# Causal attention with 8-wide heads on one core: queries and keys as two float32r parts in two 64-row halves, in place of three bf16 parts in 72 rows

## The chip, the cores and the metric

The kernel runs on one core of a Trainium2 chip. The metric is device time in microseconds; the figure given for a kernel is the median of its runs.

## The reference, cut to what matters

The program is a network of four stages in a row: an attention-like scan (attn_a), a feed-forward layer with local attention (ffn), the attention treated here (attn_b), and the second ffn layer; each adds to the same activations X of 4 batches by 1024 tokens by 128 channels. In attn_b, X is first normalised over the channels. Then, for 16 heads of 8 channels:

```python
Q = split_heads(einsum('bsd,od->bso', x, Wq)); K = ...; V = ...     # 16 heads of 8
Q, K = _apply_rope(Q, cos, sin), _apply_rope(K, cos, sin)
logits = einsum('bhnd,bhmd->bhnm', Q, K) / sqrt(8)                  # 1024 x 1024 for each head
logits = where(causal, logits, -inf)
probs = softmax(logits, axis=-1)
attn = einsum('bhnm,bhmd->bhnd', probs, V)
return einsum('bsd,od->bso', merge_heads(attn), Wo)
```

The logits must be near float32 precision, while a TensorE pass in bf16 keeps 8 bits of each factor. So the kernel splits each query and key into parts and sums the products of the parts along the rows (the contraction) of one matmul.

## The kernel before, in words

The 4 x 16 heads are treated in 16 groups of 4 heads (`NG`, `BG`). Each of the five engines has its own instruction stream, written out by hand in one order; semaphores hold the streams together. Nothing is scheduled at run time.

**Parts.** After projection and rotation, the queries and keys of a batch are split into three bf16 parts: ScalarE writes the first part (`first_part`, L1789), the remainder is formed (L1928 on VectorE for batch 0, L2036 on GpSimd for the others), ScalarE writes the second part (`second_part`, L1793), and the third is remainder minus second (`third_part`, L1933, L2041). The parts go to DRAM (`store_parts`), and are read back for each group with the repetitions that a matmul needs (`load`, L1505 and L1511, 3 DMAs of 192 KB each for queries and keys): 3 x 3 x 8 = 72 rows, for 4 heads by 1024 columns. Three further rows hold ones on the key side and, on the query side, the negated row maximum in three bf16 parts.

**Two score passes for each group.** The *maximum pass* (`max_unit`) makes query tile i (128 queries) against keys in pieces of up to 512 columns (L1652), with a causal mask added by a matmul with the identity (L1649) where the piece touches the diagonal, in one of two 512-column PSUM buffers (`s1_ps`). VectorE reduces each unit to a maximum (L1956). There are 38 units to a group. When a group's maxima are there, VectorE takes the minimum of the two halves (L1966), GpSimd splits it in three (L2063 to L2069), TensorE turns it (`turn_unit`, L1661), VectorE copies it out (L1973), and one DMA puts it into the query rows (`rows`, L1532). The *exponential pass* (`exp_unit`) makes key tile j against all later queries (L1684, 75 rows, so that the maximum is already subtracted), one head of up to 1024 columns at a time for j < 4 and two or four heads for shorter ones, in one of two 1024-column PSUM buffers (`s2_ps`); ScalarE evaluates the exponential into `PT` (L1867). There are 22 units to a group. In groups 0 to 2 the diagonal is masked by a matmul (L1679), from group 3 on (`SELECTS`) by a GpSimd select on `PT` (L2080). Then `value_block` (L1702) multiplies the probabilities by the values, in float32, in four 32-column strips of the array, one for each head. A ones column in the values gives the denominators.

**The order.** Step n has 8 slots. In slot j, TensorE makes the exponential units of key tile j of group n, between them the maximum units of group n+1 (slots 0 to 3) or n+2 (slots 4 to 7) in the order of tiles `MAX_TILES = (4, 7, 6, 5, 3, 2, 1, 0)`, and the value blocks of key tile j-1. `turn_unit` stands in slot 5. A maximum unit waits until VectorE has read the buffer before last (`s1_read`), an exponential unit until ScalarE has (`probs`):

```python
wait(pe, s1_read, k - 1)      # max_unit
wait(pe, probs, k - 1)        # exp_unit
if (j, g) == (0, 0):
    pe.wait_ge(s_rows[n % 2], 16 * (n // 2 + 1))
```

SyncE's queue issues, in step n: the outputs of the step before, `rows(n + 1)`, the outputs' first half, and `load(n + 3)`.

## Time and profile before

| | us |
|---|---|
| median of 3 runs | 2247.53 |
| the runs | 2243.55 to 2248.66 |
| span of the profiled execution, first to last instruction | 2242.3 |
| what the runs have around that span | 1.3 to 6.4 (5.2 at the median) |
| attn_b, within the span | 893 to 1503 |

The profiled execution's own device time is not given apart from its span. In the rows below, PE is TensorE's matmuls, PEld its weight loads, DVE VectorE, ACT ScalarE, POOL GpSimd, SPq the DMA queue of SyncE. A float32 matmul stands in the trace as two records, each with its own weight load. PEclk is the granted clock of TensorE as a share of full speed.

### The profile page before, as it was taken

Reading aid. Unit: us, or ns where it says so; the run is one execution under the profiler, and the core shown is the slowest. Engines: PE = TensorE matmul, PEld = TensorE weight load, DVE = VectorE, ACT = ScalarE, POOL = GpSimd, SP = SyncE. Lnnn points to the kernel's source line nnn. Section 1 sums busy time; section 2 is a strip of 40 time slices with the busy share of each in tenths; the row PEclk is TensorE's granted clock in tenths of the full one; section 3 lists DMA queues with packets and bytes.
Section 4 is the critical chain, followed back from the end, with each engine's and each line's share of the span. In section 5 each row is a group of like instructions: output and inputs, shape, how many; then the busy total and the mean of one; then the engine's idle time right before and its main releaser. Section 6 shows DMA issues by size and latency. Waiting matters only on the chain. (4 is left out here: it accounts for less than half of the span.)

```text
span 2242.3 us, 44709 instructions
## 1 busy us (share of the span) xinstructions
PE 2064.8 (92%) x16567; PEld 1059.9 (47%) x16567; DVE 1792.0 (80%) x2386; ACT 1390.5 (62%) x3475; POOL 1233.3 (55%) x633
## 2 busy tenths in 40 slices
PE   5677899999999997899999999967999999999997
PEld 2224555555555553443333333314555555555554
DVE  6986889899899993666777777717899899899993
ACT  8455566666666664446666666665666756766663
POOL 0217777777777772135121221128777787777770
PEclk9899999999999999889999999999999999999998
DMA  2004112112112110402111111113111111111111
GB/s 62 0 6 121 35 34 47 35 34 48 35 36 47 35 34 19 130 29 88 55 48 52 54 36 46 32 55 87 31 43 42 35 44 39 34 44 39 35 34 43
DMA packets 86075, 101.14 MB, mean 45 GB/s; under 512 B 13817, under 2 KB 59841, under 8 KB 83557
## 3 DMA queue, kind: packets, MB, share of 16 engines
q1 hardware_dynamic: 83429, 96.58, 16.8%
q8 instruction: 135, 2.21, 0.4%
q10 hardware_dynamic: 2432, 1.70, 0.3%
q14 instruction: 79, 0.65, 0.1%
HBM read 35.98 MB, written 8.39 MB: 20 GB/s over the span
## 5 line engine op out<-in xcount | busy, mean ns | idle before, releaser
L831 POOL TENSOR_TENSOR ffn_RN<-ffn_SS,ffn_mhalf 128x16 f32<-128x16 f32 x128 | 372.5, 2910 | 279.3 <-DVE ffn_SS L777 278.9
L1956 DVE TENSOR_REDUCE attn_b_NX<-attn_b_s 128x1 f32<-128x512 f32 (+3 forms) x608 | 381.3, 660 | 132.0 <-PE attn_b_s L1652 126.8
L825 POOL TENSOR_TENSOR ffn_QK<-ffn_T 128x1024 f32<-128x1024 f32 x128 | 421.6, 3294 | 17.6 <-DVE ffn_T L725 17.4
L576 ACT ACTIVATE ffn_PB<-ffn_s,ffn_NM 128x128 f32<-128x128 f32 x1024 | 360.8, 386 | 101.1 <-DVE ffn_NM L747 101.1
L1867 ACT ACTIVATE attn_b_PT<-attn_b_s 128x1024 f32<-128x1024 f32 (+3 forms) x352 | 298.2, 870 | 192.4 <-PE attn_b_s L1684 188.0
L612 ACT ACTIVATE ffn_SQ<-ffn_w 128x1024 f32<-128x1024 f32 x128 | 131.2, 1025 | 312.0 <-DVE ffn_T L725 311.7
L819 POOL TENSOR_TENSOR ffn_PB<-ffn_PB,ffn_RDEN 128x1024 f32<-128x1024 f32 x128 | 243.7, 1904 | 25.1 <-DVE ffn_RDEN L710 25.1
L367 PE MATMUL ffn_w<-ffn_Wqkv,ffn_H 128*128 128x512 f32 x512 | 244.2, 600 | 10.4 <-ACT ffn_SQ L612 4.7
L576 ACT ACTIVATION_READ_ACCUMULATOR ffn_PB<-ffn_s,ffn_NM 128x1 f32 x1024 | 231.0, 226 | 0.0
L1652 PE MATMUL attn_b_s<-attn_b_KS,attn_b_QS 72*128 72x512 bf16 (+3 forms) x768 | 220.6, 336 | 6.2 <-DVE attn_b_NX L1956 5.5
L741 DVE TENSOR_TENSOR ffn_QK<-ffn_QK,ffn_RN 128x1024 f32<-128x1024 f32 x128 | 222.4, 1738 | 0.4 <-POOL ffn_RN L831 0.3
L764 DVE COPY ffn_PT<-ffn_w 128x1024 f32<-128x1024 f32 x128 | 156.2, 1220 | 76.1 <-PE ffn_w L421 72.6
L2080 POOL TENSOR_SCALAR_AFFINE_SELECT attn_b_PT<-attn_b_PT 128x512 f32<-128x512 f32 x104 | 66.8, 642 | 252.6 <-ACT attn_b_PT L1867 251.4
L1684 PE MATMUL attn_b_s<-attn_b_QS,attn_b_KS 75*128 75x512 bf16 (+3 forms) x768 | 186.9, 333 | 5.9 <-ACT attn_b_PT L1867 4.8
L442 PE MATMUL ffn_m<-ffn_HN,ffn_W 128*114 128x512 f32 x360 | 185.9, 613 | 6.4 <-ACT ffn_G L596 3.7
L722 DVE TENSOR_TENSOR ffn_T<-ffn_w,ffn_rope 128x1024 f32<-128x1024 f32 x128 | 154.8, 1210 | 36.6 <-PE ffn_w L367 36.4
L1702 PE MATMUL attn_b_o<-attn_b_PT,attn_b_VQ 128*32 128x512 f32 (+3 forms) x1536 | 166.2, 505 | 3.8 <-POOL attn_b_PT L2080 3.5
L725 DVE TENSOR_TENSOR ffn_T<-ffn_w,ffn_rope 128x512 f32<-128x512 f32 x256 | 163.7, 681 | 0.0
L747 DVE TENSOR_REDUCE ffn_NM<-ffn_s 128x8 f32<-128x1024 f32 x128 | 155.6, 1215 | 9.6 <-PE ffn_s L409 9.6
L774 DVE TENSOR_REDUCE ffn_SS<-ffn_SQ 128x16 f32<-128x1024 f32 x128 | 154.6, 1208 | 2.2 <-ACT ffn_SQ L612 2.2
L437 PEld LDWEIGHTS ffn_w<-ffn_PT,ffn_Voff 128*64 128x64 f32 x2048 | 107.3, 137 | 100.7 <-issue 94.4
L421 PEld LDWEIGHTS ffn_w<-ident,ffn_PB 128*128 128x128 f32 x1024 | 117.4, 143 | 75.4 <-issue 60.5
(257 smaller groups left out, 3756.4 us busy)
## 6 DMA issues: line engine op xcount, KB each, us to landing
ffn_Voff<-ffn_Vcur SPq DMA_DIRECT2D x248, 128.0 KB, 2.3
attn_b_QS<-attn_b_qk_parts SPq DMA_DIRECT2D x48, 192.0 KB
attn_b_KS<-attn_b_qk_parts SPq DMA_DIRECT2D x48, 192.0 KB
ffn_H<-ffn_Y SPq DMA_DIRECT2D x64, 128.0 KB, 2.5
ffn_H<-ffn_U SPq DMA_DIRECT2D x64, 128.0 KB, 2.5
attn_b_qk_parts<-attn_b_RP SPq DMA_DIRECT2D x6, 768.0 KB, 4.3
ffn_rope<-in_ffn_rope_dram SPq DMA_DIRECT2D x4, 1024.0 KB, 7.9
attn_b_rope<-attn_b_OS SPq DMA_DIRECT2D x252, 16.0 KB
```

What stands on the lines that cost most here:

```text
L367: last = pe.matmul(w0_ps[:, c, :], H1[:, g % 2, b, :], Wqkv[:, l, c, :], start=True, stop=True)
L442: pe.matmul(mlp_bank(g, half, j), W1[:, g // NT, half, j, :], HN[:, :], start=True, stop=True)\
L576: last = act.activation(PB[:, x % 2, e, p, :], s_ps[:, e, p * P:(p + 1) * P], ACT.Exp, bias=NM[:, x % 2, e, p:p + 1], accum_out=DEN[:, x % ...
L741: dve.tensor_tensor(qk, qk, RN[:, x % 2, :].unsqueeze(2).broadcast_to([P, 2 * NH, DH]), ALU.mult)\
L819: pool.tensor_tensor(probs_x, probs_x, by, ALU.mult).then_inc(normed, 1)
L825: pool.tensor_tensor(QK[:, x % 2, :, :, :].rearrange("p c q k -> p (c q k)"), T1[:, :, :, :].rearrange("p c h k -> p (c h k)"), T2[:, :, : ...
L831: pool.tensor_tensor(RN[:, x % 2, :], SS[:, x % 2, :], mhalf[:, :], ALU.pow).then_inc(rnorm, 1)
L1652: last = pe.matmul(bank[:, q * width:(q + 1) * width], QS[0:KS9, m % RING, g + q, i * P:(i + 1) * P], KS[0:KS9, m % RING, g + q, lo:hi], s ...
L1684: last = pe.matmul(bank[:, q * pitch + lo:q * pitch + hi], KS[:, n % RING, g + q, j * P:(j + 1) * P], QS[:, n % RING, g + q, j * P + lo:j ...
L1702: last = pe.matmul(o_ps[half][VCOLS * g:VCOLS * (g + 1), lo - half * 512:512], VQ[:, n % 2, g, j, :], PT[:, j % 2, g, lo - j * P:hi - j * ...
L1867: act.activation(PT[:, j % 2, g:g + pack, 0:width], s2_ps[k % 2][:, 0:pack * pitch].rearrange("p (q w) -> p q w", q=pack)[:, :, 0:width], ...
L1956: dve.tensor_reduce(NX[:, m % 2, c, g:g + pack, i], s1_ps[k % 2][:, 0:pack * (hi - lo)].rearrange("p (q w) -> p q w", q=pack), AX_X, ALU.m ...
```

## The change

The number of parts falls from three to two, and their type becomes float32r with 12 significant bits each (`PARTS = 2`, a 4-byte type). A pair of parts now needs 2 x 2 x 8 = 32 rows (`TERMS`), with one row of ones against zeros and two rows for the maximum 35 in all, so two heads fit one above the other: heads of parity 0 in rows 0 to 63, of parity 1 in rows 64 to 127 (`NPAR`, `HROWS`, `rows_for`).

- Maximum pass: a unit is still one 512-column buffer and one reduction, now of one parity; units alternate between the parities. The four pieces of 128 columns of tile 4's second half join the four of tile 0 in two units. 38 units as before. The mask of a diagonal piece is two matmuls of 64 rows and 64 columns a piece instead of one of 128 rows and 128 columns.
- Exponential pass: a unit is now two heads (one of each parity) by one half of the queries, each head in its own 512-column bank of the 1024-column buffer; 20 units to a group instead of 22. In groups 0 to 2 there are four mask matmuls to a masked unit.
- Parts: `second_part`, `third_part` and, of `offsets`, two of the four GpSimd operations go. The remainder is written straight into the second part.
- The turn is a float32 matmul. `rows` becomes four DMAs of one row each instead of one of three rows. `load` becomes 8 DMAs of 128 KB instead of 6 of 192 KB; `store_parts` carries 8 KB for each channel instead of 6 KB. The ones come from four GpSimd fills at the start instead of three DMAs.

```diff
-PARTS = 3
-KS9 = PARTS * PARTS * BD
+PARTS = 2
+TERMS = PARTS * PARTS * BD
+NPAR, NPR = 2, 2
+HROWS = P // NPAR
...
-        RP = sb("RP", [P, 2, PARTS, T], BF16)
+        RP = sb("RP", [P, 2, PARTS, T], F32R)
-        QS = sb("QS", [KS9 + PARTS, RING, BG, T], BF16)
-        KS = sb("KS", [KS9 + PARTS, RING, BG, T], BF16)
+        QS = sb("QS", [P, RING, NPR, T], F32R)
+        KS = sb("KS", [P, RING, NPR, T], F32R)
...
         def max_units(slot):
             i = MAX_TILES[slot]
-            return [(i, c, g, pack) for c in range(i // 4 + 1) for g, pack in max_heads(i, c)]
+            if i == 0:
+                return [(par, P, [(0, 0, pr) for pr in range(NPR)] + [(4, 1, pr) for pr in range(NPR)])
+                        for par in range(NPAR)]
+            units = []
+            for c in range(1 if i <= 4 else 2):
+                packed = (i, c) in ((1, 0), (5, 1))
+                width = min(512, (i + 1) * P - c * 512)
+                for group in ([range(NPR)] if packed else [[pr] for pr in range(NPR)]):
+                    units += [(par, width, [(i, c, pr) for pr in group]) for par in range(NPAR)]
+            return units
+
+        def exp_units(j):
+            units = []
+            for half in range(j // 4, 2):
+                n = NPR if piece(j, half)[1] - piece(j, half)[0] <= 256 else 1
+                units += [(half, pr, n) for pr in range(0, NPR, n)]
+            return units
...
             def rows(m):
                 sp.wait_ge(s1_read, s1_at["turn", m] + 1)
-                sp.dma_start(QS[KS9:KS9 + PARTS, m % RING, :, :].rearrange("a g t -> a (g t)"), MT[:, m % 2, :])\
-                  .then_inc(s_rows[m % 2], 16)
+                for par in range(NPAR):
+                    for a in range(PARTS):
+                        at = par * HROWS + TERMS + 1 + a
+                        of = (a * NPAR + par) * NPR * NT
+                        sp.dma_start(QS[at:at + 1, m % RING, :, :].rearrange("a q t -> a (q t)").bitcast(F32),
+                                     MT[of:of + NPR * NT, m % 2, :]).then_inc(s_rows[m % 2], 16)
...
+            def mask(at, par, kind, half, n, first):
+                rows = rows_for(par, HROWS)
+                pe.matmul(at, causal[rows, kind, half, 0:P],
+                          causal[rows, kind, half:half + 1, P:P + HROWS].broadcast_to([HROWS, n, HROWS]), start=first,
+                          stop=True, skip_group_check=True)
...
-                for q in range(pack):
-                    last = pe.matmul(bank[:, q * width:(q + 1) * width], QS[0:KS9, m % RING, g + q, i * P:(i + 1) * P],
-                                     KS[0:KS9, m % RING, g + q, lo:hi], start=not diagonal, stop=True,
+                rows = rows_for(par, TERMS + 1)
+                for q, (i, c, pr) in enumerate(segments):
+                    last = pe.matmul(bank[:, q * width:(q + 1) * width], QS[rows, m % RING, pr, i * P:(i + 1) * P],
+                                     KS[rows, m % RING, pr, c * 512:c * 512 + width], start=not diagonal, stop=True,
...
                 for q in range(pack):
-                    for lo in range(0, width, 512):
-                        hi = min(width, lo + 512)
-                        last = pe.matmul(bank[:, q * pitch + lo:q * pitch + hi],
-                                         KS[:, n % RING, g + q, j * P:(j + 1) * P],
-                                         QS[:, n % RING, g + q, j * P + lo:j * P + hi],
+                    for par in range(NPAR):
+                        rows = rows_for(par, TERMS + 1 + PARTS)
+                        last = pe.matmul(bank[par][:, q * width:(q + 1) * width],
+                                         KS[rows, n % RING, first + q, j * P:(j + 1) * P],
+                                         QS[rows, n % RING, first + q, lo:hi], start=not masked and q == 0, stop=True,
                                          skip_group_check=True)
...
-            for w in range(2):
-                second_part(0, w)
...
             def remainder(w):
-                dve.wait_ge(p1, w + 1)
+                dve.wait_ge(upper, w + 1)
                 dve.wait_ge(rsum, w + 1)
-                dve.tensor_tensor(TA[:, w, :], TA[:, w, :], RP[:, w, 0, :], ALU.subtract).then_inc(r1, 1)
+                dve.tensor_tensor(RP[:, w, 1, :], TA[:, w, :], RP[:, w, 0, :].bitcast(F32), ALU.subtract)\
+                   .then_inc(lower, 1)
...
-            pool.memset(zeros[:, :], 0.0).then_inc(s_set, 1)
+            pool.memset(zeros[:, :, :], 0.0).then_inc(s_set, 1)
+            for par in range(NPAR):
+                at = par * HROWS + TERMS
+                pool.wait_ge(s_set, 2 * par + 1)
+                pool.memset(KS[at:at + 1 + PARTS, :, :, :].bitcast(F32), 1.0).then_inc(s_set, 1)
+                pool.wait_ge(s_set, 2 * par + 2)
+                pool.memset(QS[at:at + 1, :, :, :].bitcast(F32), 0.0).then_inc(s_set, 1)
```

## Rows read from the trace of the kernel before

**Rows 1.** The page's head: busy time, share of the span, instructions.
```profile
PE 2064.8 (92%) x16567; PEld 1059.9 (47%) x16567; DVE 1792.0 (80%) x2386; ACT 1390.5 (62%) x3475; POOL 1233.3 (55%) x633
```

**Rows 2.** Stretches of attn_b: PE, PEld, DVE, ACT, POOL busy (instructions), clock, DMA share, GB/s.
```profile
975.90:1011.60 35.70, 34.80 (x199) 13.50 (x199) 24.56 (x42) 18.26 (x22) 8.21 (x8) 0.76 0.01 2
...
1043.80:1080.00 36.20, 34.51 (x244) 13.46 (x242) 24.55 (x41) 22.89 (x29) 9.76 (x9) 0.91 0.27 86
1080.00:1460.90 380.90, 364.32 (x2588) 131.42 (x2585) 293.13 (x489) 238.70 (x301) 76.16 (x153) 1.00 0.16 44
```

**Rows 3.** Timeline: the turn's copy, in two neighbouring steps (start, duration, us).
```profile
1239.09 0.28 DVE L1973 CAST attn_b_MT<-attn_b_s 96x128 bf16<-96x128 f32 x1
...
1270.45 0.28 DVE L1973 CAST attn_b_MT<-attn_b_s 96x128 bf16<-96x128 f32 x1
```

**Rows 4.** Waits from 1110 to 1420 us: total us, times, longest.
```profile
ACT attn_b_PT L1867 <- PE attn_b_s L1684: 111.1, 121, 2.9
PEld attn_b_s L1649 <- DVE attn_b_NX L1956: 74.2, 144, 0.8
DVE attn_b_NX L1956 <- PE attn_b_s L1652: 66.8, 126, 0.8
```

**Rows 5.** Timeline of slot 0: exponential and maximum units in turn.
```profile
1245.18 3.77 ACT L1867 ACTIVATE attn_b_PT<-attn_b_s 128x1024 f32<-128x1024 f32 x4 [1.00 <-PE attn_b_s L1684]
...
1247.17 0.61 PE L1684 MATMUL attn_b_s<-attn_b_QS,attn_b_KS 75*128 75x512 bf16 x2
1247.62 0.38 PE L1652 MATMUL attn_b_s<-attn_b_KS,attn_b_QS 72*128 72x512 bf16 x1
```

**Rows 6.** Timeline of slots 1 to 4: value blocks, masks, reductions.
```profile
1254.52 0.22 PE L1649 MATMUL attn_b_s<-attn_b_causal,identb 128*128 128x128 bf16 x1
1254.58 0.38 PE L1652 MATMUL attn_b_s<-attn_b_KS,attn_b_QS 72*128 72x512 bf16 x1
...
1257.60 2.34 DVE L1956 TENSOR_REDUCE attn_b_NX<-attn_b_s 128x1 f32<-128x512 f32 x4 [0.39 <-PE attn_b_s L1652]
1260.70 4.41 DVE L1956 TENSOR_REDUCE attn_b_NX<-attn_b_s 128x1 f32<-128x384 f32 x7 [0.76 <-PE attn_b_s L1652]
...
1264.31 1.07 PE L1702 MATMUL attn_b_o<-attn_b_PT,attn_b_VQ 128*32 128x512 f32 x8
1265.31 0.28 PE L1649 MATMUL attn_b_s<-attn_b_causal,identb 128*128 128x256 bf16 x1
```

**Rows 7.** Timeline of TensorE in the ffn stage: float32, whole array and quarters.
```profile
599.34 1.04 PE L386 MATMUL ffn_w<-ident,ffn_QK 128*128 128x128 f32 x8
...
601.07 1.88 PE L367 MATMUL ffn_w<-ffn_Wqkv,ffn_H 128*128 128x512 f32 x4
...
605.49 1.04 PE L409 MATMUL ffn_s<-ffn_KT,ffn_QT 64*64 64x128 f32 x32
```

**Rows 8.** Groups by shape: weight loads, busy us, mean ns | idle before.
```profile
L386 PEld LDWEIGHTS ffn_w<-ident,ffn_QK 128*128 128x128 f32 x1024 | 116.6, 143 | 22.9 <-issue 16.1 <-DVE ffn_QK L741 2.3
...
L1684 PEld LDWEIGHTS attn_b_s<-attn_b_QS,attn_b_KS 75*128 75x128 bf16 x768 | 67.7, 100 | 63.5 <-ACT attn_b_PT L1867 29.0 <-issue 5.7
```

**Rows 9.** Timeline of the stage's start: parts of batch 0, squares of chunk 4, fills.
```profile
914.10 1.04 ACT L1793 ACTIVATE attn_b_RP<-attn_b_TA 128x1024 bf16<-128x1024 f32 x1
...
916.45 1.07 ACT L1774 ACTIVATE attn_b_PT<-attn_b_s 128x512 f32<-128x512 f32 x2
...
915.37 2.43 DVE L1933 TENSOR_TENSOR attn_b_RP<-attn_b_TA,attn_b_RP 128x1024 bf16<-128x1024 f32 x2
...
893.87 1.80 POOL L2015 MEMSET attn_b_VQ<- 128x2048 f32 x1
```

**Rows 10.** Timeline of SyncE's queue after the turn, and the next step's first unit.
```profile
1239.39 0.78 SPq L1532 DMA_DIRECT2D attn_b_QS<-attn_b_MT  x1
...
1240.29 2.66 SPq L1523 DMA_DIRECT2D attn_b_rope<-attn_b_OS  x4
...
1244.54 0.60 PE L1684 MATMUL attn_b_s<-attn_b_QS,attn_b_KS 75*128 75x512 bf16 x2
```

More of the change, by code:

```diff
@@ L1669, in exp_unit @@
+                pe.matmul(s1_ps[k % 2][0:PARTS * BG * NT, 0:P],
+                          NP[:, m % 2, :, :, :, :].rearrange("p a g h i -> p (a g h i)").bitcast(F32),
+                          keep["ident"][:, :], start=True, stop=True).then_inc(s1_mm, 1)
+            def exp_unit(n, j, u):
+                k = s2_at[n, j, u]
+                half, first, pack = exp_units(j)[u]
+                lo, hi = piece(j, half)
+                width = hi - lo
                 wait(pe, probs, k - 1)
-                if (n, j, g) == (0, 0, 0):
+                if (n, j, u) == (0, 0, 0):
@@ L1724, in step @@
                     halves = list(range(j // 4, 2)) if 0 <= v < NG else []
-                    pieces, done = len(heads) + len(halves), 0
+                    pieces, done = len(exps) + len(halves), 0
                     def some_maxima(done):
-                        for unit in scores[len(scores) * done // pieces:len(scores) * (done + 1) // pieces]:
-                            max_unit(m, *unit)
+                        for u in range(len(scores) * done // pieces, len(scores) * (done + 1) // pieces):
+                            max_unit(m, slot, u)
@@ L1738, in step @@
                             value_block(v, j, halves[0])
                             done = some_maxima(done)
-                        if halves and k == len(heads) - 1:
+                        if halves and u == len(exps) - 1:
                             value_block(v, j, halves[-1])
                             done = some_maxima(done)
-                    if not heads:
-                        for unit in scores[:1]:
-                            max_unit(m, *unit)
+                    if not exps:
+                        for u in range(len(scores))[:1]:
+                            max_unit(m, slot, u)
@@ L1746, in step @@
                         if slot == TURN_SLOT and n == -1:
                             turn_unit(0)
-                        for unit in scores[1:]:
-                            max_unit(m, *unit)
+                        for u in range(len(scores))[1:]:
+                            max_unit(m, slot, u)
                             if m == 0:
@@ L1834, in _ @@
             hold(2, 0)
-            for w in range(2):
-                second_part(1, w)
             hold(2, 1)
@@ L1942, in _ @@
             remainder(1)
-            for w in range(2):
-                third_part(w)
             for c in range(4, NCH):
@@ L2160, in causal_masks @@
 def causal_masks(np):
-    low = np.tril(np.ones((P, P), bool))
-    return np.where(np.stack([low, low.T], 1), 0.0, -3e38)
+    r = np.arange(HROWS)[:, None]
+    c = np.arange(HROWS)[None, :]
+    m = np.zeros((HROWS, 2, 2, P + HROWS))
+    low, high, cut = m[..., 0:HROWS], m[..., HROWS:P], m[..., P:]
+    low[:, 0, 0] = r == c
+    cut[:, 0, 0] = -3e38 * (c > r)
+    high[:-1, 0, 1] = (r == c)[:-1]
+    low[-1, 0, 1] = 1.0
+    cut[:, 0, 1] = -3e38 * (c > r)
+    cut[-1, 0, 1] = -3e38
+    low[1:, 1, 0] = (r == c)[1:]
+    high[0, 1, 0] = 1.0
+    cut[:, 1, 0] = -3e38 * (c < r)
+    cut[0, 1, 0] = -3e38
+    high[:, 1, 1] = r == c
+    cut[:, 1, 1] = -3e38 * (c < r)
+    return np.concatenate([m, m], 0)
 def band_masks(np):
@@ L2245 @@
         "attn_b_rope": rope_tables(np)[by_row],
-        "attn_b_ones": np.ones((PARTS, T), np.float32).astype(bf16),
         "attn_b_WqT": a["attn_b_Wq"][by_row].T,
```

279 lines of the change are left out of this document (128 added, 151 removed).

## The prediction

> **What bounds the kernel now.** I read the page's head first: TensorE is busy 92% of the span, VectorE 80% [rows 1]. That is a mean over four stages, and the change touches one, so next come the stretches of attn_b [rows 2]. In the twelve steps from 1080 to 1460.9 us TensorE is busy 364.3 of 380.9 us (96%), VectorE 293.1 (77%), ScalarE 238.7 (63%), GpSimd 20%. Two neighbouring copies of the turned maxima are 31.36 us apart [rows 3]: that is an ordinary step, and there are about 15 of them. The waits say the same from the other side [rows 4]: ScalarE waits 111 us for exponential matmuls and VectorE 67 us for maximum matmuls, while TensorE waits for buffers in pieces of 0.8 us at most. So TensorE sets the step.
>
> "Busy" is not "streaming", though: what remains of a matmul after its last column hides short waits. I count columns. Each pass makes 4 heads x 36 tile pairs x 128 = 18,432 columns in a step, the masks 4,096. A 1024-column exponential unit takes 0.45 us from its start to the next instruction's [rows 5], so 0.22 us for 512 columns. Exponential pass 7.9 us, maximum pass 7.9, masks 1.7. Value blocks: 1.00 us for 512 columns of four heads [rows 6]; the 12 of a step (six of 512, two each of 384, 256 and 128) come to about 9.4 us. Sum 26.9 of 31.4 us; the other 4.5 are waits of TensorE, shown or hidden. They have two places. In slot 0 ScalarE evaluates four units back to back in 3.77 us [rows 5]: there ScalarE paces. In slots 1 to 4 VectorE takes four to seven reductions in a row and then waits 0.4 to 0.8 us for the unit behind a value block [rows 6]: there TensorE paces.
>
> **The change, part by part.** All sizes are for one ordinary step unless it says otherwise.
>
> *Exponential matmuls.* Two heads in two row halves, each to a bank of its own. No float32r instruction and no 64-row by 128-column pair stands in the trace, so this is bounded from rows. For overlap: 32 float32 records of 128 columns in quarters of the array take 1.04 us, 0.027 us each after the 0.17 us tail, while eight on the whole array take the same 1.04 us, 0.107 each [rows 7]. Four quarters do overlap fully, and two of the four are row halves. For the rate: a float32 record takes 0.43 us for 512 columns (four in 1.88 us [rows 7]), two records to a matmul, so 0.85 us; bf16 takes 0.22. Float32r lies between 0.22 and 0.85 us for 512 columns. I take 0.22: float32's fourfold price is that of making high and low halves of both factors, and a 12-bit part has no low half. The nearest row by width, a single float32 record at 0.43, is kept for a rival. So 7.9 us becomes 3.95: -3.95, bounds -3.95 and +7.7 (four passes, overlapped).
>
> The Trainium skill speaks to this rate (FP8 and Floating Point Precision, TensorE Precision Notes): a reduced-precision mode reads 4-byte floats and cuts them to 22 bits, and true float32 is four passes. By it one pass serves, as taken; no run here has shown it yet.
>
> *What of it is on the path.* In slot 0 ScalarE's 3.6 to 3.8 us stay, so of that slot's 0.9 us saved only some 0.25 counts: +0.65.
>
> *Masks.* Per step 22 mask matmuls become 44, with the same columns in all. A mask of 128 columns takes 0.06 us before the score matmul follows [rows 6], which is just its columns; each of the 22 added ones costs between nothing and 0.06: 0 to +1.3. I take 0.03 each, the time of 64 columns: +0.7.
>
> *Weight loads.* 48 float32r loads for each pass. A float32 load of 128 columns reads 143 ns, a bf16 one 100 [rows 8]. Where the matmul lasts 0.22 us it is hidden. Eight float32 records of 128 columns, each with its load, follow at 0.107 us [rows 7], so a hidden load costs 0.107 at most. It is bare behind the short masks of 22 diagonal units and in the eight 128-column pieces: 30 x 0 to 0.08, or 0 to +2.4. I take +0.5, near the low end, because quarters reload at 0.027 us without showing it [rows 7].
>
> The Trainium skill's rule here speaks against the change (TensorE: Matmul & The Clock Gate, Weight-path perf modes): fast weight load is on for 128 weights unless the type is float32, and a plain load takes columns / 1.2 (its section LDWEIGHTS), an estimate of 107 ns. By it the term would be about +2 in place of +0.5; by the rows the answer is open.
>
> *Maximum matmuls.* Units alternate between the halves, so two in a row can overlap when both buffers are free. After each of the six value blocks of slots 1 to 3 two units follow and both buffers are free by then: up to 6 x 0.22 = -1.3. But then VectorE holds the next unit, so I take half: -0.6.
>
> *VectorE, ScalarE, GpSimd.* 38 reductions as before, exponentials of the same elements in 20 instead of 22 instructions, two GpSimd operations fewer. None paces except ScalarE in slot 0. VectorE's 24.1 us busy is the floor below any gain.
>
> *DMA and what is queued.* `rows` now issues four DMAs. Four small ones take 2.66 us to issue where the single one takes 0.78 [rows 10]. The exponential unit that waits for them starts 5.2 us after the turn's copy (1239.37 to 1244.54), and on TensorE everything behind it waits too. New: 2.7 us of issue and about 2 us to land, 4.7 of 5.1. It just fits: 0, bound +1. The stores and loads behind it in SyncE's queue start 1.9 us later and have over a step to spare, since the ring is three groups deep.
>
> Sum: -3.95 + 0.65 + 0.7 + 0.5 - 0.6 = -2.7. A step of 28.7 us, bounds 27.2 to 31.
>
> *Outside the steps.* At the start ScalarE's two second parts (from 914.10) hold back the squares of chunk 4 at 916.45, and VectorE's third parts end at 917.8 [rows 9]; chunks 4 to 7 and so the first maximum unit follow from there: -2.3. The later batches lose a ScalarE pair and 4 us of GpSimd: -0.7. The four new fills are of 6,144 elements in few rows; at 1.80 us for 2,048 [rows 9] they take 4 x 5.4 = 22 us from 894 on, done by 918, before the first unit at 931 that waits for them. If that cover were gone they would cost their excess. The last step has no maxima and is paced by ScalarE and GpSimd in turn: -1.5 (0 to -4).
>
> In all 15 x -2.7 - 3 - 1.5 = -45 on the span of 2242.3: 2197.3. The median of the runs stands 5.2 us above that span: 2202.5, say 2203. A difference of 0.2% (4.5 us) is about what a measurement of this kernel can tell from no change.
>
> **The rivals.**
> 1. *The smaller costs come at their upper ends.* Pieces of 128 columns cost what float32 does, 0.21 instead of 0.05 (8 in the maximum pass and 4 overlapped pairs in the exponential pass: +1.9), or loads at +2.4, or rows late by 1. For: nothing shows them cheap. Against: they would have to stand in the TensorE-bound slots. With +1.5 a step: 2203 + 22 = 2225.
> 2. *No overlap of the halves, at full rate.* The exponential pass stays at 7.9, masks and loads are added: +1.3 a step, 31.4 to 32.7. 15 x 1.3 - 4.5 = +15: 2263. For: only quarters are shown, never 64 x 128. Against: the same rows. It turns the sign once less than a third of the pair's time overlaps (the 1.2 of added cost against 3.95).
> 3. *Float32r streams like a float32 record.* 0.43 us for 512 columns: the exponential pass is where it was, the maximum pass rises by 7.9 less some overlap of 2, masks and loads add 1: about +6.6 a step, 15 x 6.6 - 4.5 = +94: 2342. With all four passes the maximum pass alone rises by 23 us: about +28 a step, 2670. For: the only 4-byte rows. Against: two parts of 12 bits. VectorE would wait several us a slot.
> 4. *The clock.* The steps at 975.9 and 1043.8 run at 0.76 and 0.91 of the clock and take 35.7 and 36.2 us [rows 2], although TensorE is 95 to 97% busy. With TensorE lighter and the array half filled it might fall more often; at a mean of 0.93 over the stage, streaming grows by some 2 us a step: 2233.
>
> **How the numbers follow.** The forecast 0.62 (own range 2180 to 2222), rival 1 0.14, rival 2 0.08, rival 3 0.10, rival 4 0.06. The range goes from 27.2 us a step with the last step's full gain (15 x -4.2 - 7 = -70, so 2177, and some margin: 2172) up to 2255, past rivals 1 and 4; rivals 2 and 3, 0.18, stay out. Faster: the forecast, 1 and 4, less their edges, 0.79. Within 0.2%: 0.03, between rivals 1 and 2. Slower: 0.18.
>
> **What would show it.** Right: the copies of the turned maxima 28.7 us apart; two float32r records of 512 columns starting within a few ns of one another, and the next instruction 0.22 us on; one record to a matmul; VectorE's busy share up from 77% to 84% at an unchanged 24 us a step; a wait of ScalarE for L1684's heir about 3 us a step shorter; the first reduction near 930. Wrong: starts 0.2 us apart (rival 2); records of 600 ns (rival 3); 128-column records as long as 300 ns or gaps behind the masks (rival 1); a granted clock below 1.00 in ordinary steps (rival 4); the first exponential unit of a step released by the rows' DMA.

## The result, and the profile after

| | before | after |
|---|---|---|
| median, us | 2248.1 (2243.55 to 2254.05, 4 runs) | 2534.2 (2529.28 to 2534.91, 4 runs) |
| span of the profiled execution | 2242.3 | 2527.5 |

The kernel became slower: ratio 1.126, 95% interval 1.124 to 1.129. 2203 was forecast, with a range up to 2255.

The head and the 40 slices of the page of the changed kernel (each digit tenths of a slice of 63 us; PEclk is the granted clock of TensorE):

```profile
PE 2329.4 (92%) x16998; PEld 1206.3 (48%) x16998; DVE 1797.8 (71%) x2383; ACT 1380.4 (55%) x3435; POOL 1234.5 (49%) x599
...
DVE  7967989898999546544454454452489989899994
...
PEclk9899999999999987555555555555799999999999
```

TensorE's share is 92%, as in [rows 1], and tells nothing. PEclk is the row that changed: half of full speed, so 1.2 GHz in place of 2.4, from the first turn of maxima at 982.6 us to the end of attn_b. Up to that turn the clock is the same in both (0.89 and 0.88 from 932 to 975 us; until 893 us TensorE is busy 802.9 and 803.4 us), and the second ffn layer runs at its old clock again (0.99 from 1790 us).

The stretches of attn_b after the change (columns as in [rows 2]), the turns' copies as in [rows 3], and the waits of 1300 to 1600 us as in [rows 4]:

```profile
982.50:1734.30 751.80, 709.35 (x3672) 310.52 (x3671) 374.70 (x608) 296.16 (x341) 98.66 (x149) 0.50 0.12 30
1300.00:1400.00 100.00, 93.44 (x484) 40.55 (x476) 49.33 (x80) 38.56 (x44) 11.85 (x22) 0.50 0.11 27
```

```profile
1227.87 0.28 DVE L1986 COPY attn_b_MT<-attn_b_s 64x128 f32<-64x128 f32 x1 [0.31 <-PE attn_b_s L1685]
...
1277.73 0.28 DVE L1986 COPY attn_b_MT<-attn_b_s 64x128 f32<-64x128 f32 x1 [0.32 <-PE attn_b_s L1685]
```

```profile
ACT attn_b_PT L1891 <- PE attn_b_s L1709: 183.2, 89, 6.4
DVE attn_b_NX L1973 <- PE attn_b_s L1676: 147.1, 153, 2.0
```

An ordinary step is 49.9 us (1277.73 - 1227.87), where it was 31.4 and where 28.7 was forecast. The fifteen steps take 751.7 us against 485.0 before: 266.7 of the 285.2 us. The rest: 6.6 us by the first turn (982.55 against 975.9), 7.7 in the last step (from the last turn to the output projection 44.6 us against 36.9), 4 behind it. VectorE does its 24 us of reductions a step, as before, but now waits about half the time, each wait up to 2.0 us.

Now the matmuls themselves. Timeline of TensorE, and below it the groups of the page (total busy, mean ns):

```profile
1400.71 0.79 PE L1676 MATMUL attn_b_s<-attn_b_KS,attn_b_QS 33*128 33x512 f32 x2
1401.31 0.63 PE L1709 MATMUL attn_b_s<-attn_b_QS,attn_b_KS 35*128 35x512 f32 x2
...
1403.74 1.93 PE L1726 MATMUL attn_b_o<-attn_b_PT,attn_b_VQ 128*32 128x512 f32 x8
```

```profile
L1676 PE MATMUL attn_b_s<-attn_b_KS,attn_b_QS 33*128 33x512 f32 (+3 forms) x768 | 358.2, 620 | 16.4 <-DVE attn_b_NX L1973 14.7
L1709 PE MATMUL attn_b_s<-attn_b_QS,attn_b_KS 35*128 35x512 f32 (+3 forms) x768 | 270.7, 587 | 9.2 <-ACT attn_b_PT L1891 9.0
```

768 records are 48 pieces in 16 groups: one record to a matmul, not two as for float32. Two exponential matmuls of 512 columns are over in 0.63 us together, tail included, at half clock; at the same clock one bf16 matmul of 512 columns alone reads 0.60 (1301.25 us in the run with 35 rows, below). So the instruction does what the forecast took it to do: one pass, at the rate of bf16, two heads at once. But everything on TensorE has nearly doubled, the value blocks too, which the change does not touch: 1.93 us against 1.07 in [rows 6].

### The profile page after: what moved, and what is told of

The parts are those of the page before. It is cut to its first block and busy times, and to the rows that moved or that the text cites. A ratio compares the mean times of both kernels' runs of the same rounds, so it can differ in the third digit from the quotient of the medians.

```text
span 2527.5 us, 45562 instructions
## 1 busy us (share of the span) xinstructions
PE 2329.4 (92%) x16998; PEld 1206.3 (48%) x16998; DVE 1797.8 (71%) x2383; ACT 1380.4 (55%) x3435; POOL 1234.5 (49%) x599
## 5 line engine op out<-in xcount | busy, mean ns | idle before, releaser
L1973 DVE TENSOR_REDUCE attn_b_NX<-attn_b_s 128x1 f32<-128x512 f32 (+3 forms) x608 | 387.5, 661 | 385.7 <-PE attn_b_s L1676 385.1
L1891 ACT ACTIVATE attn_b_PT<-attn_b_s 128x1024 f32<-128x1024 f32 (+1 forms) x320 | 294.5, 938 | 472.5 <-PE attn_b_s L1709 472.5
L1676 PE MATMUL attn_b_s<-attn_b_KS,attn_b_QS 33*128 33x512 f32 (+3 forms) x768 | 358.2, 620 | 16.4 <-DVE attn_b_NX L1973 14.7
L615 ACT ACTIVATE ffn_SQ<-ffn_w 128x1024 f32<-128x1024 f32 x128 | 131.0, 1024 | 315.1 <-DVE ffn_T L728 314.8
L1726 PE MATMUL attn_b_o<-attn_b_PT,attn_b_VQ 128*32 128x512 f32 (+3 forms) x1536 | 289.3, 847 | 0.6 <-POOL attn_b_PT L2090 0.5
L1709 PE MATMUL attn_b_s<-attn_b_QS,attn_b_KS 35*128 35x512 f32 (+3 forms) x768 | 270.7, 587 | 9.2 <-ACT attn_b_PT L1891 9.0
L1676 PEld LDWEIGHTS attn_b_s<-attn_b_KS,attn_b_QS 33*128 33x128 f32 x768 | 180.3, 304 | 119.5 <-DVE attn_b_NX L1973 87.2
L1709 PEld LDWEIGHTS attn_b_s<-attn_b_QS,attn_b_KS 35*128 35x128 f32 x768 | 151.4, 314 | 57.8 <-ACT attn_b_PT L1891 49.7
```

What stands on the lines that cost most here:

```text
L1676: last = pe.matmul(bank[:, q * width:(q + 1) * width], QS[rows, m % RING, pr, i * P:(i + 1) * P], KS[rows, m % RING, pr, c * 512:c * 512 + ...
L1709: last = pe.matmul(bank[par][:, q * width:(q + 1) * width], KS[rows, n % RING, first + q, j * P:(j + 1) * P], QS[rows, n % RING, first + q ...
L1726: last = pe.matmul(o_ps[half][VCOLS * g:VCOLS * (g + 1), lo - half * 512:512], VQ[:, n % 2, g, j, :], PT[:, j % 2, g, lo - j * P:hi - j * ...
L1891: act.activation(out, bank, ACT.Exp).then_inc(probs, 1)
L1973: dve.tensor_reduce(at, bank, AX_X, ALU.max, negate=True).then_inc(s1_read, 1)
```

## The experiments

Two questions stand open. Why is the clock granted at half, and what would the change have been worth at the full clock? The theories for the first:

- *Rows*: the score matmuls now use 33 or 35 of the array's 128 rows where they used 72 and 75 (the named cause, though not the size, of the prediction's rival 4).
- *Type*: float32r itself.
- *Pairs*: two matmuls at once in two halves.
- *Idleness*: TensorE waits more.

### Few rows alone, in the kernel before

The products of the third parts are left out (so the scores have fewer bits): the kernel before, all in bf16 and with no halves, with 32 and 35 rows.

```diff
-KS9 = PARTS * PARTS * BD
+SUMS = 2
+KS9 = SUMS * SUMS * BD
...
-                for a in range(PARTS):
-                    at = slice(a * PARTS * BD, (a + 1) * PARTS * BD)
+                for a in range(SUMS):
+                    at = slice(a * SUMS * BD, (a + 1) * SUMS * BD)
```

> The kernel before (bf16, whole-array addressing, no halves) with the products of the third bf16 part left out: score matmuls over 32 and 35 rows instead of 72 and 75, 4 part DMAs instead of 6 for each group; everything else the same. Theory A (few rows lower the clock): the clock falls to about 0.5 in the steps of attn_b, a step goes from 31.4 to 50 us or more, the time to some 2560 to 2620. Theory B (type or mode): clock 1.00 and 2248 as before.

Measured: 2704.3 us (one run), more than expected. Its 1080 to 1850 us, nearly thirteen steps:

```profile
1080.00:1850.00 770.00, 770.00 (x2748) 160.95 (x2740) 323.55 (x510) 258.80 (x315) 79.49 (x153) 0.50 0.06 15
```

Ordinary steps of 60.5 us, the clock at 0.50, and TensorE without a gap in its records. No float32r and no pair of halves is in it, so neither is needed. It rules out idleness as the cause too: here an engine whose records fill 100% of 770 us is not given its full clock. The Trainium skill describes the clock as going by how busy TensorE has been (TensorE: Matmul & The Clock Gate, Part 1, "What's actually happening"); this trace disagrees as far as busy means occupied time. The step is 60.5 us at half clock and was 31.4 at full, nearly twice as long: at half clock TensorE sets it.

### The halves in bf16

The changed kernel with bf16 tiles for the parts; still 33 and 35 rows, still in pairs (the scores lose bits again).

```diff
-        QS = sb("QS", [P, RING, NPR, T], F32R)
-        KS = sb("KS", [P, RING, NPR, T], F32R)
+        QS = sb("QS", [P, RING, NPR, T], BF16)
+        KS = sb("KS", [P, RING, NPR, T], BF16)
```

> The changed kernel with all of its float32r tiles in bf16: the parts keep 8 bits each instead of 12, so precision is left out, and the DMAs carry half of the bytes; 33 and 35 rows in two halves as in the changed kernel. Theory A (few rows): clock 0.50, steps near 50 us, about 2520. Theory B for the type float32r: clock 1.00, steps 28 to 30 us, about 2200. Theory B for the two-halves mode: clock 0.50.

Measured: 2432.7 us (one run), the clock 0.50 to 0.61 over a step, most steps at 0.50 and 44.5 us (2520 and 50 were expected). So the type is not needed for the fall of the clock here either. It has a price of its own: 49.9 against 44.5 us a step, both at 0.50.

### Sixty-four rows in each half

The changed kernel, float32r and pairs kept. The rows above the 35 take part too, holding zeros on the query side and ones on the key side, so that the sums stay the same. GpSimd clears three rows again for each group.

```diff
-                rows = rows_for(par, TERMS + 1)
+                rows = rows_for(par, HROWS)
...
-                        rows = rows_for(par, TERMS + 1 + PARTS)
+                        rows = rows_for(par, HROWS)
...
-                pool.memset(KS[at:at + 1 + PARTS, :, :, :].bitcast(F32), 1.0).then_inc(s_set, 1)
+                pool.memset(KS[at:at + HROWS - TERMS, :, :, :].bitcast(F32), 1.0).then_inc(s_set, 1)
...
-                pool.memset(QS[at:at + 1, :, :, :].bitcast(F32), 0.0).then_inc(s_set, 1)
+                pool.memset(QS[at:at + HROWS - TERMS, :, :, :].bitcast(F32), 0.0).then_inc(s_set, 1)
```

> The changed kernel with every score matmul over all 64 rows of its half (rows 35 to 63 hold ones on the key side and zeros on the query side; GpSimd zeroes the three rows with the old maxima before a group's maximum pass). Same columns, same instructions on TensorE, results unchanged. Theory A (the granted clock fell to 0.50 because the score matmuls use only 33 or 35 rows of the array's 128): more rows bring the clock back, fully or in part; at 1.00 the steps are 28 to 30 us and the time is 2190 to 2230. Theory B (the float32r type, or the two-halves mode, is what the clock does not honour): the clock stays at 0.50 and the time at 2534. Theory C (rows count only where they hold values other than zero): stays at 2534 too.

Measured: 2303.5 us (2302.05 to 2307.6), 1.025 of before, interval 1.023 to 1.027. Rows that add only zeros to the sums take 231 us off the changed kernel. The 2190 to 2230 us of the expectation were not reached, since the clock is back only in part and a step at full clock is not as short as was thought. Here are the page's slices of the granted clock, and two stretches: one ordinary step at full clock, and one of the bouts at half clock that remain.

```profile
PEclk9899999999999999989999779998999999999999
```

```profile
1449.30:1482.50 33.20, 28.13 (x241) 12.72 (x240) 24.28 (x41) 21.54 (x27) 9.59 (x13) 1.00 0.18 41
1268.00:1296.00 28.00, 26.13 (x130) 9.98 (x127) 14.96 (x25) 11.37 (x14) 6.54 (x7) 0.53 0.19 44
```

Ordinary steps at full clock take 33.1 us (four of the fifteen; two more at full clock take 33.8 and 35.5), those with bouts at half clock up to 45.5.

### Sixty-four rows in one of the two passes

Each of the two `rows` edits above alone (the fills at the start stay; the clearing comes with the maximum pass, which alone needs it).

```diff
-                        rows = rows_for(par, TERMS + 1 + PARTS)
+                        rows = rows_for(par, HROWS)
```

> The changed kernel with 64 rows per half in the exponential pass alone (zeros against ones in the added rows); the maximum pass keeps its 33. Theory 'rows that take part set the clock': about half of the score columns of a step now use 64 rows and half 33, so the clock should lie between the 0.50 of the changed kernel and the 0.84 to 1.00 of the run with 64 rows in both passes; total between 2303 and 2534 us, about 2420, with a step between 34 and 50 us. Rival 'what lets the clock fall are the pairs of overlapped matmuls': those are all in the exponential pass and stay overlapped, so the clock stays at 0.50 and the total at about 2534. Rival 'the maximum pass alone decides': also 2534.

Measured: 2482.4 us (one run); steps of 43.5 to 51.4, nearly full 50 where the clock stays down. The forecast of 2420 was too low, the order right. The other half:

```diff
-                rows = rows_for(par, TERMS + 1)
+                rows = rows_for(par, HROWS)
```

> The counterpart of the run with 64 rows in the exponential pass alone: here the maximum pass uses 64 rows and the exponential pair 35 each. Theory 'both passes count alike': the clock is 0.50 with short bouts above it and the step near that run's 43.5 to 50 us, total about 2480. Rival 'one pass decides': if the maximum pass is the one that keeps the clock up, it stays at 0.84 or more and the step at 33 to 36 us, total near 2303.

Measured: 2450.8 us (one run, 2480 expected), steps of 34.4 to 49.9. The same 360 us, 1080 to 1440, of the run with the exponential pass filled, and then of the one with the maximum pass filled:

```profile
1080.00:1440.00 360.00, 336.83 (x1779) 145.43 (x1779) 183.28 (x297) 145.09 (x169) 38.51 (x72) 0.53 0.15 36
```

```profile
1080.00:1440.00 360.00, 331.75 (x1886) 143.58 (x1884) 194.17 (x318) 153.72 (x179) 69.55 (x93) 0.59 0.13 34
```

With neither pass filled the mean clock is 0.50, with one 0.53 or 0.59, with both 0.88 over the same stretch. Both passes count, neither decides. The pairs are there in all four, at 0.50 as at 0.88, so they do not bring the clock down by themselves.

### All rows in the kernel before

Before, the clock already dipped in two steps [rows 2]. Here the kernel before has zeros in the rows above 75 and takes all 128 rows in the exponential pass; the maximum pass keeps its 72 (the expectation below names the scores in general, but only this pass was changed). The two fills of 10.3 us on GpSimd end at 917.6, ahead of its first work on batch 0 at 926.

```diff
-        QS = sb("QS", [KS9 + PARTS, RING, BG, T], BF16)
-        KS = sb("KS", [KS9 + PARTS, RING, BG, T], BF16)
+        QS = sb("QS", [P, RING, BG, T], BF16)
+        KS = sb("KS", [P, RING, BG, T], BF16)
...
+            pool.memset(QS[64:P, :, :, :], 0.0).then_inc(fills, 1)
+            pool.wait_ge(fills, 2)
+            pool.memset(KS[64:P, :, :, :], 0.0).then_inc(fills, 1)
```

> The kernel before, its scores' contraction carried over all 128 rows: rows above the third part hold zeros. Theory 'rows that take part set the clock': the two early dips, 0.76 in the step from 975.9 us and 0.91 in the step from 1043.8 us, go away, those steps fall from 35.7 and 36.2 to about 32 us and the total by 4 to 8 us (2240 to 2244), less the some 15 us that the two zero fills may put on the start. Rival 'the dips come from the pauses of TensorE at the start of the stage': they stay at 0.76 and 0.91 with the steps at 35 to 36 us.

Measured: 2238.45 us (2233.49 to 2239.84, 6 runs), 0.996 of before, interval 0.994 to 0.997. The two steps that dipped:

```profile
978.90:1010.30 31.40, 30.36 (x199) 11.94 (x199) 24.36 (x42) 17.91 (x22) 8.23 (x8) 0.89 0.01 2
1042.50:1075.70 33.20, 31.36 (x244) 12.53 (x242) 24.39 (x42) 22.98 (x29) 9.77 (x9) 1.00 0.29 93
```

Their clock rises from 0.76 and 0.91 to 0.89 and 1.00, and they take 31.4 and 33.2 us where they took 35.7 and 36.2: 7.3 us, without one matmul fewer. All other steps are as before to 0.1 us. But the second of the two proves nothing. In the run below that leaves exponential columns out from group 3 on, the instructions up to there are those of the kernel before, and there the first dip stays and the second is missing:

```profile
977.10:1014.40 37.30, 36.38 (x198) 13.75 (x199) 24.51 (x41) 18.29 (x21) 8.18 (x8) 0.73 0.01 2
1046.60:1079.80 33.20, 31.38 (x245) 12.52 (x242) 24.37 (x41) 22.93 (x29) 9.77 (x9) 1.00 0.29 93
```

The first dip, and the mean clock over whole executions, carry the reading: 0.974 to 0.979 in the six with 128 rows, 0.967 to 0.974 in thirteen of the kernel before. So the number of rows moved the clock in the kernel before too. The added rows hold zeros on both sides here.

### Halves of 64 rows in bf16

What are the halves worth, with the clock held and no float32r? The kernel of 64 rows a half with bf16 tiles (fewer bits in the scores). One run took 2236.6 us; the same kernel was then run six times more:

> The 64-row kernel with its float32r tiles in bf16 (8-bit parts, precision left out). It takes only the float32r weight load away. In the 64-row kernel a score matmul of 512 columns whose load cannot run ahead reads 0.50 us, against 0.39 where it can: 0.107 us bare. If that load is what a clean step pays over the kernel before, clean steps fall from 33.1 to 31 us or below and a pair of 512 columns takes 0.24 us to the next instruction in place of 0.34. If the loss lies in the order of the units, steps stay at 33. The clock as in the 64-row kernel.

> Halves of 64 rows in both passes with queries and keys in three bf16 parts' layout cut to two bf16 tiles, as in the earlier single look at 2236.6 us (the float32r values are rounded to bf16, so the scores are less exact). Theory 'halves alone give 0.5 to 0.7 us a step once the clock holds and the loads are the fast ones': 2248 - 15 x 0.7 - 2 = about 2236, ratio 0.993 to 0.997. Rival 'the single look was noise': ratio within 0.2% of 1.

Measured: 2235.9 us (2233.9 to 2240.65, 6 runs), 0.995 of before, interval 0.994 to 0.997. One ordinary step:

```profile
1263.70:1294.40 30.70, 25.02 (x239) 7.74 (x237) 23.66 (x41) 21.31 (x27) 9.60 (x13) 1.00 0.12 28
```

Two readings. Against the float32r step of the same rows and clock, the type costs 33.1 - 30.7 = 2.4 us a step. Against the step before, the halves with two parts gain 31.4 - 30.7 = 0.7 us, although TensorE's busy share between 1080 and 1440 us falls from 96% (344.2 of 360) to 82% (294.5). Where each goes is the matter of the last experiments.

### Where float32r's 2.4 us lie

Timeline of an exponential pair and the maximum unit behind it, with their weight loads, in the two kernels of 64 rows; first float32r:

```profile
1267.70 0.50 PE L1709 MATMUL attn_b_s<-attn_b_QS,attn_b_KS 64*128 64x512 f32 x2 [0.18 <-ACT attn_b_PT L1893]
1268.04 0.39 PE L1676 MATMUL attn_b_s<-attn_b_KS,attn_b_QS 64*128 64x512 f32 x1
...
1267.70 0.18 PEld L1709 LDWEIGHTS attn_b_s<-attn_b_QS,attn_b_KS 64*128 64x128 f32 x2 [0.62 <-ACT attn_b_PT L1893]
1267.80 0.19 PEld L1676 LDWEIGHTS attn_b_s<-attn_b_KS,attn_b_QS 64*128 64x128 f32 x1
```

Then bf16:

```profile
1270.56 0.39 PE L1709 MATMUL attn_b_s<-attn_b_QS,attn_b_KS 64*128 64x512 bf16 x2 [0.89 <-ACT attn_b_PT L1893]
1270.79 0.38 PE L1676 MATMUL attn_b_s<-attn_b_KS,attn_b_QS 64*128 64x512 bf16 x1
...
1270.55 0.10 PEld L1709 LDWEIGHTS attn_b_s<-attn_b_QS,attn_b_KS 64*128 64x128 bf16 x2 [1.25 <-ACT attn_b_PT L1893]
1270.57 0.10 PEld L1676 LDWEIGHTS attn_b_s<-attn_b_KS,attn_b_QS 64*128 64x128 bf16 x1
```

Both pairs start as soon as ScalarE frees the buffer. The float32r pair holds TensorE for 0.34 us (1267.70 to 1268.04), the bf16 one for 0.23. The difference, 0.11 us, goes with where the third load starts: 0.10 us behind the first two in float32r, 0.02 in bf16. The first load stands bare because it carries the wait for the buffer itself (its idle time is put down to ScalarE), so it did not run ahead. The Trainium skill gives columns / 1.2 ns for a load (TensorE: Matmul & The Clock Gate, "LDWEIGHTS (loading the stationary operand)"), an estimate of 107 ns for 128 columns: the 0.10 us of float32r agrees. Its section "Weight-path perf modes" takes only FP32 out of the fast mode; these float32r loads read 182 to 189 ns where bf16 loads of the same shape read 92 to 96, so they don't show it.

Over a whole step of each kernel, the times from one matmul's start to the next add up to 12.25 and 10.60 us for the exponential pieces, 9.92 and 8.99 for the maximum pieces, 1.18 and 1.47 for the masks: 1.65 + 0.93 - 0.29 = 2.3 of the 2.4 us. These times hold waits as well as loads; how much of them is bare load was not measured apart.

If only the load were the matter, would it help to let the score matmul go first in a diagonal unit, with its masks behind?

```diff
-                if diagonal:
-                    at = bank[:, 0:n * width].rearrange("p (q w) -> p q w", q=n)
-                    for half in range(2):
-                        lo = width - P + half * HROWS
-                        mask(at[:, :, lo:lo + HROWS], par, 0, half, n, half == 0)
                 rows = rows_for(par, HROWS)
                 for q, (i, c, pr) in enumerate(segments):
...
+                if diagonal:
+                    at = bank[:, 0:n * width].rearrange("p (q w) -> p q w", q=n)
+                    for half in range(2):
+                        lo = width - P + half * HROWS
+                        last = mask(at[:, :, lo:lo + HROWS], par, 0, half, n, False)
```

> The changed kernel with 64 rows per half in both passes, and in the diagonal units the score matmul ahead of its two 64-column masks in place of behind them. Theory 'the float32r load stands bare': the load of the 128 weights (0.11 us bare, of a 0.18 us record) can then run under the matmul ahead of the unit; of 22 diagonal units of a step about half are on the path, so the clean step at clock 1.00 falls from 33.1 to about 32.2 us. Rival 'the step is set by the hand over of the two maximum buffers': 33.1 stays 33.1 within 0.2. The total moves less than the clock's bouts do, so the steps at full clock decide.

Measured: 2296.8, 2298.1 and 2303.7 us (a fourth execution, at a lower clock, took 2352.0), ratio 1.023, interval 1.021 to 1.025. Later steps at full clock take 33.1 to 33.9 us where the kernel of 64 rows has 33.1: no gain. The expectation's rival held. The load does not come to stand under the matmul ahead of the unit, since it now waits for the buffer itself. The longest waits of one step (1407.1 to 1440.7):

```profile
PEld attn_b_s L1671 <- DVE attn_b_NX L1975: 12.3, 19, 1.0
```

These are nineteen loads for scores that stand behind VectorE's release: a load of 0.18 us is bare there, where in the diagonal units it was the mask's of 0.09. In this kernel, then, a load is hidden only when its buffer has come free before.

### Where the halves' gain went

In the kernel before, from group 3 on, exponential units of j < 4 do only their first 512 columns (5,120 columns a step are left out, 2.1 us at 0.22 us for 512 and 0.43 for 1,024).

```diff
-                    for lo in range(0, width, 512):
+                    for lo in range(0, width if n < SELECTS or j >= 4 else 512, 512):
```

> The kernel before with the second 512-column chunk of the exponential matmuls of key tiles 0 to 3 left out from group 3 on (ScalarE still evaluates the whole buffer, old scores in that part): 5,120 of 18,432 exponential columns fewer, 2.1 us of TensorE a step, all in slots 0 to 3. Theory S: steps fall by 1.3 to 2.1 us, total 2225 or less. Theory L: steps fall by 0 to 0.5 us, total 2240 to 2248, with TensorE idle by that much more. If the clock follows TensorE's activity it may dip in some steps.

Measured: 2241.9 us (one run, so the total is no measure; the steps repeat to 0.1 us). An ordinary step falls from 31.4 to 30.8: of 2.1 us taken from TensorE 0.6 count. The waits of 1080 to 1440 us in this run:

```profile
ACT attn_b_PT L1867 <- PE attn_b_s L1684: 126.8, 131, 2.7
PEld attn_b_s L1649 <- DVE attn_b_NX L1956: 97.8, 168, 0.8
DVE attn_b_NX L1956 <- PE attn_b_s L1652: 73.0, 136, 0.9
```

TensorE waits more for VectorE (97.8 against 84.6 us before, same window), and VectorE still waits 73.0 (76.5). Exponential columns mostly fill time in which TensorE would otherwise stand before a full maximum buffer; take them away, and that wait shows instead. VectorE's own waits might come from the 1.0 us value blocks, during which it has read both buffers. That was tried too, by cutting value blocks above 256 columns in two, with maximum units between the pieces (the second piece of a block then starts its sums anew, so part of the accumulation is left out):

```diff
-            def value_block(n, j, half):
+            def value_block(n, j, half, part=0, of=1):
...
+                mid = (half + 1) * 512 - 256
+                lo, hi = (lo, hi) if of == 1 else ((lo, mid), (mid, hi))[part]
```

> The kernel before, with each value block of more than 256 columns issued as two pieces with a maximum unit between them; nothing else. Theory L (in slots 1 to 4 the step is paced by the handshake of TensorE and VectorE over the two maximum buffers: VectorE finishes its two filled buffers inside a value block of 1.0 us and then waits 0.7 us, and exponential columns are not on that path): pieces of 0.6 us end most of that wait, some 0.3 to 0.5 us at each of 8 blocks, so a step falls from 31.4 to 28.5 to 30 us and the time to 2205 to 2235. Theory S (TensorE's streamed columns pace the step, as the prediction had it): eight more switches of 0.1 us make the step 0.5 to 1 us longer, 2255 to 2262. The clock stays at 1.00 in ordinary steps by both.

> The 64-row kernel with the value blocks in two pieces in the same way. Theory L: clean steps fall from 33.1 to 29 to 31 us; the clock, which fell below 1.00 in a third of the steps, is higher or the same; 2210 to 2270. Theory S: 33.1 stays or rises, 2300 to 2315.

Measured: in the kernel before 2268.5 us (2261.9 to 2275.37), 1.010 (1.008 to 1.012), ordinary steps 31.5; in the kernel of 64 rows 2284.3 (2280.68 to 2286.84), 1.016 (1.014 to 1.017), against 1.025 whole. Neither came down to the 28.5 to 31 us a step of the theory that was to be tried. In the first, 10.6 of the 17.9 us that its profiled span is longer are two early steps at a lower clock (42.3 us at 0.64 and 40.2 at 0.83). In the second, the third step, at full clock in both kernels, takes 32.6 us where it took 33.8 with whole blocks: there the cut gives something. In the first, VectorE waits as long as before, in smaller pieces:

```profile
DVE attn_b_NX L1965 <- PE attn_b_s L1652: 73.8, 246, 0.9
```

That is 0.30 us each against 0.53 (76.5 in 145). TensorE is now busy 353.8 of 360 us, where it was 344.2; the added loads and changes may have eaten what the shorter blocks gave. So the waits follow the order of the blocks. That the length of a value block sets the step is not shown, since the cut put more work on TensorE as well.

## Why the prediction was wrong

**The step that failed: rival 4, the clock, which was priced at 0.93 of full speed and given 0.06.** The prediction named the mechanism ("with TensorE lighter and the array half filled it might fall more often") and read the sign of it, two early steps at 0.76 and 0.91 with TensorE 95 to 97% busy [rows 2]. It did not ask what those dips said: an engine that is busy that much and yet loses its clock loses it for something other than pauses, and the change halves the rows used. Over the fifteen steps the mean was 0.50 and not 0.93. Put together for an ordinary step: 31.4, less 0.7 for the halves, plus 2.4 for float32r, plus 49.9 - 33.1 = 16.8 for the clock, makes 49.9. Fifteen times 16.8 is 252 of the 285 us. The 33.1 is a step of the kernel with 64 rows a half, GpSimd's clearing included, and stands in for the changed kernel at full clock, which no run shows. (The fifteen steps before held some 14 us more than 15 x 31.4, the early dips among them.)

The terms of the sum, which would have mattered at full clock:

- *Exponential matmuls, -3.95.* The rate and the overlap were right: one record to a matmul, two starts within 5 ns, 0.23 us to the next instruction in bf16 halves. (Not in each pair: in an ordinary step of the bf16 halves 12 of the 24 pairs start within 14 ns, and 8 are 0.20 to 0.28 us apart, because the second half still has a matmul in it.) That all but the share of slot 0 lies on the path was wrong. Halves at full clock gave 0.7 us in all, and 2.1 us taken from TensorE in another way gave 0.6. "TensorE sets the step", read from 96% busy, was the mistake: most exponential columns stand where TensorE would otherwise wait for a maximum buffer. The hand-over of the two maximum buffers between TensorE and VectorE is the likeliest bound of slots 1 to 4; it is argued from the waits and not shown.
- *Weight loads, +0.5.* The rise from bf16 to float32r is 2.4 us, and the load is the only difference on TensorE that the rows show. The prediction's own upper end was +2.4. The row of quarters that reload at 0.027 us misled: those loads are of 64 columns, these of 128, and many of them wait for their buffer first. The estimate of about +2, from the Trainium skill's rule (TensorE: Matmul & The Clock Gate, Weight-path perf modes), was nearer.
- *Masks, +0.7, and pairs in the maximum pass, -0.6.* They were not taken apart by a run. From one matmul's start to the next, the masks add up to 1.94 us in a step before and to 1.47 in the bf16 halves, so the 22 added ones cost nothing; the maximum pieces to 10.02 and 8.99, waits included.
- *Rows' DMAs, 0.* Right. The four mostly take 2.44 us to issue; in the bf16 halves the next step's first exponential unit starts 5.24 us after the turn's copy starts (1263.61 to 1268.85), where it was 5.45 (1239.09 to 1244.54), and the trace puts no wait down to them.
- *Outside the steps, -3 - 1.5.* The start did not come forward: the first pair of reductions is at 932.50, before at 932.13, though ScalarE's second parts are gone and its squares of chunks 4 and 5 come at 915.16 and 916.73 instead of back to back from 916.45. ScalarE now waits there for TensorE's centring matmul, so its second parts had held back little:

```profile
916.73 0.60 ACT L1800 ACTIVATE attn_b_PT<-attn_b_s 128x512 f32<-128x512 f32 x1 [0.98 <-PE attn_b_s L1584]
```

From the first reduction to the first turn it takes 50.0 us, before 43.8, at the same clock. The prediction has no term for this. In the bf16 halves it is 47.5, so the halves cost 3.7 and the type 2.6. In this stretch maximum units stand between projections on the whole array, and each change between a whole-array and a half-array matmul costs some 0.09 us. Before, then bf16 halves:

```profile
953.44 1.02 PE L1591 MATMUL attn_b_s<-attn_b_XN,attn_b_W 128*128 128x512 f32 x2
954.30 0.22 PE L1649 MATMUL attn_b_s<-attn_b_causal,identb 128*128 128x128 bf16 x1
```

```profile
954.30 1.12 PE L1606 MATMUL attn_b_s<-attn_b_XN,attn_b_W 128*128 128x512 f32 x2
955.36 0.39 PE L1676 MATMUL attn_b_s<-attn_b_KS,attn_b_QS 64*128 64x512 bf16 x2
```

The projection's pair of records holds TensorE for 0.86 us (953.44 to 954.30) before and for 1.06 (954.30 to 955.36) between two changes. There are 41 such changes up to the turn in the halves and none before; 41 x 0.09 is the 3.7 us. In ordinary steps they cost nothing new, since the value blocks, on strips of 32 columns, make the same changes in both kernels. The last step took 7.7 us more, at a clock of 0.50 where it was 0.91.

Rivals 2 and 3 are refuted by the records. Of rival 1's costs the loads came at their upper end (+2.4), the masks at nothing, and pieces of 128 columns follow each other at 0.11 us (kernel of 64 rows, from 1264.89 us), not at 0.21; the gain that they stood against was not there.

What stays open: what in the array is counted when the clock is granted. Rows of zeros against ones keep the clock up, so it is the rows that an instruction uses and not the values alone. But with 64 rows float32r still has bouts at 0.5 (mean 0.88 from 1080 to 1440 us), and bf16 has almost none (1.00). Why the type matters there no run tells. The runs of one execution that the account of the clock rests on differ from the kernel before by 8 to 20%, far more than executions of one kernel differ from each other; the 30 us between the two one-pass runs is read as no more than an order.

## What to carry to other kernels

A matmul on 64 or 75 rows takes as long as one on 128 (0.22 us for 512 columns), but a stretch made of matmuls on few rows may lose half of TensorE's clock, and then the full ones in it nearly double too. So look at the granted clock of the stretch before touching the shape of its matmuls: dips where TensorE is busy are a warning, and filling the unused rows with zeros, on one side at least, is a cheap remedy (2534.2 to 2303.5 us in the changed kernel, a ratio of 0.996 in the kernel before). And a busy share of 96% does not make an engine the bound: take some of its work away in one run, and see how much of it counts, before counting a gain in columns.

## What the runs showed of the hardware

- The granted clock depends on the rows that matmuls use. At 32 to 35 rows it is 0.50 with TensorE busy 100% of 770 us in bf16; at 72 and 75 rows 1.00 with an early dip to 0.76; at 72 and 128 rows that dip shrinks to 0.89. Halves of 33 and 35 rows have 0.50, of 64 rows 0.88 in float32r and 1.00 in bf16 (1080 to 1440 us). Rows of zeros count.
- Float32r matmuls stand as one record each and stream as bf16 does: a pair of 512 columns is done in 0.34 us from start to next start, 0.11 of it the bare load, and a bf16 pair in 0.23. Two halves that are both free start within 5 ns of each other.
- A float32r load of 128 columns reads 182 to 189 ns at full clock, and the load behind it starts 0.10 us later; a bf16 one reads 92 to 96 ns, and the next starts 0.02 later.
- A weight load that carries the wait for a buffer does not run ahead of it (19 loads of one step, 12.3 us of waiting), so a stream that is short of buffers pays for such loads.
- A change between a whole-array and a half-array matmul costs some 0.09 us: 512 columns of float32 on the whole array hold TensorE for 0.43 us before another whole-array matmul and for 0.53 before a half-array one.
